# A three-layer Perceiver block on one core: self outputs moved one step on, the router a part later, the last key added first

## What is computed

```python
x = x + cross(layernorm(x), ctx, mask)     # softmax(Q K^T / 4, masked) V, with biases, then Wo
x = x + self_(layernorm(x))                # rope, causal softmax attention within a sequence, then W_O
h = layernorm(x)                           # the router and the experts read h
logits = h @ router_w                      # 8 experts, top 2, capacity 32 in groups of 128 tokens
x = x + combine(wo_e @ (gelu(w0_e @ dispatch(h)) * (w1_e @ dispatch(h))))
```

## Time and profile before

| | |
|---|---|
| median of 3 runs | 516.66 us (516.65 to 517.7) |
| the profiled execution | 520.1 us, of which the span from first to last instruction 518.3 |
| TensorE busy | 486.1 us, 94% |
| VectorE busy | 391.1 us, 75% |
| ScalarE busy | 323.0 us, 62% |
| GpSimd busy | 271.7 us, 52% |
| chain that ended last | TensorE 82%, VectorE 5%, ScalarE 4%, transfers 4%, issue 4% |

### The profile page before, as it was taken

One profiled execution on the slowest core, in us unless ns is written; L12 is line 12 of the kernel. 1 busy time (PEld: TensorE's weight loads), 2 busy tenths in 40 slices (PEclk: granted clock), 3 DMA queues, 4 the chain that ended last, 5 costly groups with the idle time before them and its releaser, 6 DMA issues.

```text
span 518.3 us, 18402 instructions
## 1 busy us (share of the span) xinstructions
PE 486.1 (94%) x6699; PEld 455.4 (88%) x6699; DVE 391.1 (75%) x987; ACT 323.0 (62%) x838; POOL 271.7 (52%) x362
## 2 busy tenths in 40 slices
PE   1898999899899999999998689999999999999997
PEld 1777889889889898998987679999999999999996
DVE  2544546476677768777679988999989999999984
ACT  1456776576667767776782356666667666666651
POOL 4125443445245464444544364998666666667660
PEclk9978999899899999999999997999999999999999
DMA  6614121111111111010005400556655646456302
GB/s 178 196 49 120 23 44 44 25 44 43 24 44 21 41 41 41 21 41 21 4 4 170 159 2 1 179 163 230 188 171 173 189 139 205 133 194 204 123 1 82
DMA packets 58126, 48.92 MB, mean 94 GB/s; under 512 B 20942, under 2 KB 49744, under 8 KB 58064
## 3 DMA queue, kind: packets, MB, share of 16 engines
q1 hardware_dynamic: 58064, 48.09, 31.7%
HBM read 46.86 MB, written 1.08 MB: 92 GB/s over the span
## 4 chain that ended last, share of the span: by engine, by line
PE 82%; DVE 5%; issue 4%; ACT 4%; DMA 4%; SPq 1%; DVEq 0%; POOL 0%; ACTq 0%; POOLq 0%
PE bank L226 20%; PE bank L228 19%; PE bank L227 19%; PE bank L647 4%; PE bank L669 3%; PE bank L615 3%; PE bank L572 3%; DMA ctx_raw<-in_ctx 2%; ACT Pr L1158 1%; DMA w_raw<-in_L_xattn_Wk 1%; PE bank L1054 1%; PE bank L933 1%; PE bank L805 1%; PE bank L765 1%; PE bank L537 1%
## 5 line engine op out<-in xcount | busy, mean ns | idle before, releaser
L226 PE MATMUL bank<-XT_lo,W_hi 128*128 128x256 f32 (+1 forms) x352 | 99.3, 282 | 0.3 <-DVE XT_lo L1934 0.3
L227 PE MATMUL bank<-XT_hi,W_lo 128*128 128x256 f32 (+1 forms) x352 | 99.0, 281 | 0.0
L228 PE MATMUL bank<-XT_hi,W_hi 128*128 128x256 f32 (+1 forms) x352 | 98.8, 281 | 0.0
L2337 POOL TENSOR_TENSOR W_lo<-raw,W_hi 128x256 fp32r<-128x256 f32 (+1 forms) x88 | 84.3, 958 | 7.0
L2219 POOL TENSOR_TENSOR Pr<-Pr,rinv 128x1028 f32<-128x1028 f32 (+2 forms) x32 | 60.4, 1889 | 49.2 <-DVE rinv L1514 48.5
L1158 ACT ACTIVATE Pr<-Sc,nmax 128x257 f32<-128x257 f32 x128 | 64.5, 505 | 29.3 <-DVE nmax L1503 24.8
L1974 DVE TENSOR_TENSOR W_lo<-raw,W_hi 128x512 fp32r<-128x512 f32 (+1 forms) x88 | 71.8, 817 | 4.9 <-ACT W_hi L1335 1.2
L2335 POOL CAST W_hi<-raw 128x256 fp32r<-128x256 f32 (+1 forms) x88 | 43.5, 494 | 53.4 <-PE bank L228 32.8
L1503 DVE CUSTOM_DVE_ANT_0 Sc<-bank,mask_add 128x257 f32<-128x257 f32 x128 | 47.0, 422 | 31.0 <-PE bank L615 17.4
L2146 DVE TENSOR_TENSOR hid_lo<-hid,hid_hi 128x256 fp32r<-128x256 f32 (+1 forms) x88 | 68.7, 781 | 1.5 <-ACT hid_hi L1410 1.5
L226 PEld LDWEIGHTS bank<-XT_lo,W_hi 128*128 128x128 f32 (+1 forms) x352 | 65.4, 186 | 0.4 <-issue 0.4
(11 more groups left out here) (248 smaller groups left out, 1342.8 us busy)
## 6 DMA issues: line engine op xcount, KB each, us to landing
raw<-in_L_ffn_w_kernel SPq DMA_DIRECT2D x32, 512.0 KB, 4.6
ctx_raw<-in_ctx SPq DMA_DIRECT2D x32, 256.0 KB, 2.8
raw<-in_L_ffn_wo_kernel SPq DMA_DIRECT2D x16, 512.0 KB, 5.7
raw<-in_L_ffn_w_kernel SPq DMA_DIRECT2D x16, 344.0 KB
last_prob<-Pr SPq DMA_DIRECT2D x128, 1.0 KB, 1.8
raw<-in_L_ffn_wo_kernel SPq DMA_DIRECT2D x8, 256.0 KB
x_sb<-in_x SPq DMA_DIRECT2D x4, 256.0 KB, 5.5
VL_all<-vl_rows SPq DMA_DIRECT2D x8, 128.0 KB
```

What stands on the lines that cost most here:

```text
L226: pe.matmul(dst, a_hi, b_lo, start=first, stop=False)
L227: pe.matmul(dst, a_lo, b_hi, start=False, stop=False)
L228: return pe.matmul(dst, a_hi, b_hi, start=False, stop=last)
L2337: po.tensor_tensor(W2_lo[0:w, m % RW, :], raw2[0:w, t, :], f(W2_hi[0:w, m % RW, :]), ALU.subtract)\
```

## The change

For tiles 0 to 4 it moves `self_outputs` from the end of part 3 to part 0 of the next step, behind `outputs`, with `split_self` on ScalarE and VectorE. `project_out` moves behind `keys` of that part, VectorE's addition and statistics behind `spread_queries`; y moves from part 0 to part 1, and with it `turn_router`, ScalarE's copy yTf and GpSimd's casts; the logits move from part 1 to part 2. `add_last` comes ahead of `invert_sums` in part 2 (and waits, for bank 7, for yTf instead of the logits). The waits of `outputs` follow these moves.

```diff
             if exists(t, TT):
-                for read in (("b_oT_hi", "b_oT_lo"), ("c_yT",), ("c_lg",))[(r + 2) % 4]:
-                    pe.wait_ge(sm[read], t + 1)
+                if r != 2:
+                    pe.wait_ge(sm[("c_yT", "c_lg", None, "b_x2")[r]], t + 1)
...
-                outputs(b - 2, (u - 2) % 4, j - 3 if u < 3 else -1)
+                outputs(b - 2, (u - 2) % 4, j - 3)
...
                 if u == 0:
-                    project_out(j - 3)
+                    self_outputs(j - 3)
...
                 if u == 0:
+                    project_out(j - 3)
                     turn_qk(j - 2)
                 if u == 1:
                     after_self(j - 2, True)
+                    turn_router(j - 3)
+                elif u == 2:
                     logits(j - 3)
-                elif u == 2:
                     project_cross(j - 1)
...
-                if u == 0:
-                    turn_router(j - 3)
-                elif u == 1:
+                if u == 1:
                     turn_last(j - 1)
-                elif u == 3:
-                    self_outputs(j - 2)
...
                 if u == 0:
                     keep_self_values(j - 2)
+                    split_self(j - 3)
...
-                if u == 1:
+                if u == 2:
                     keep_logits(j - 3)
                 keep_probs(b - 1, (u - 1) % 4)
-                if u == 0:
+                if u == 1:
                     keep_router(j - 3)
-                if u == 1:
                     self_exp(j - 2)
                     keep_last(j - 1)
-                if u == 3:
+                if ending:
                     split_self(j - 2)
...
-                ve.wait_ge(sm["c_lg"], min(t - 1, EARLY) if isinstance(t, int) else t - 1)
+                if isinstance(t, int) and t == TT - 1:
+                    ve.wait_ge(sm["c_lg"], EARLY)
+                else:
+                    ve.wait_ge(sm["c_yT"], t - 1)
...
-                invert_sums(b - 1, (u - 1) % 4)
                 if u == 2:
                     add_last(j - 1)
+                invert_sums(b - 1, (u - 1) % 4)
...
                 if u == 0:
-                    add_and_norm(j - 3, "c", 0)
+                    split_self(j - 3)
...
                 if u == 0:
+                    spread_queries(j - 2)
+                    add_and_norm(j - 3, "c", 0)
+                if u == 1:
                     add_and_norm(j - 3, "c", 1)
-                    spread_queries(j - 2)
-                if u == 1:
                     shift_scores(j - 2)
...
                     rotate(j - 1)
-                    split_self(j - 2)
...
                 if u == 0:
                     power(j - 3, "c")
+                elif u == 1:
                     keep_normed(j - 3)
```

## The result

The changed kernel takes 522.74 us (median of 14 runs), the kernel before, run with it, 517.24: a ratio of 1.011, 95% interval 1.0089 to 1.0132, some 5.5 us slower. The prediction was 518.8 (515.4 to 520.6): slower was right, the size was not, 2.1 us forecast where 5.5 came. The profiled execution took 523.45 us (span 521.7) where that of before took 520.1 (518.3).

A forecast was written before the change was run, and what follows sets the result against it. TensorE's stream was taken to bound the middle of the pipeline (busy 30.12 of 30.24 us). Terms -5.65 + 4.45 - 0.70 + 2.79 + 1.80 - 0.57 = +2.1 us on the median 516.66 gave 518.8, range 515.4 to 520.6.

The forecast's parts named there:

- the new wait for y: Part 1, steps 4 to 6: the router's transposes wait 0.93 us for VectorE's y, 3 x 0.93 = +2.79.
- Part 3 loses L805: Part 3, steps 2 to 6: the self outputs leave, with idle around them, 5 x -1.13 = -5.65 us.
- L805's place: Bounds on moving the self outputs from part 3 to part 0: -1.0 to +0.65 us on the sum.
- +0.89: Part 0: 1.01 for L805, -0.22 for the router transposes, +0.1 of waiting; five times, +4.45 us.
- The wait of project_out for O2T_lo: Part 0: TensorE waits 0.1 us for VectorE's O2T_lo, from 0 to 0.2.
- +0.17: Part 2 per step: gains the logits, 0.36 us, and loses the 0.19 wait for OT.
- The wait for OT: Part 2, before outputs (L669): the 0.19 us wait goes in three steps, -0.57; bound: it stays.
- one for PT (1.0): Part 1's outputs might wait for VectorE's late copy of PT: taken as 0, at most 0.2 us a step.
- half clock in steps 4 to 6: Rival: new waits are followed by half clock, 520.3 us for one such stretch, 523.3 for three; chance 0.09.
- wait-free version: Rival: the wait for y in part 1 isn't there, 516.0 us, or 515.0 with L805 at its lower bound; chance 0.12.
- the tail: Rival: after the pipeline, the half-clock stretch from 310.50 to 317.00 us doesn't occur, 515.5 us; chance 0.10.
- The gap of the first pass: Rival: the 1.90 us gap in part 1 of step 3 shrinks by 0.89 and the clock may hold, 517.3; chance 0.07.

The follow-up runs named there:

- The router's half alone: Kernel before with only y, its transposes, copies and casts moved to part 1 and the logits to part 2; self outputs stay: 521.08 us, ratio 1.0071.
- The pair of KT runs: ScalarE's KT made directly behind the spread self probabilities (PTd) in part 3: in the changed kernel 520.70 us, in the kernel before 516.69 us.
- last_T first: Kernel before with ScalarE's last_T made ahead of the exponential of the self scores in part 1: 517.89 us, ratio 1.0015.
- the run with that alone: Kernel before with only VectorE's addition of the last key moved ahead of the reciprocal of the sums: 517.79 us, ratio 1.0004.
- three kernels that keep the order of before on TensorE: Kernel before with one edit each: KT directly behind PTd 516.69 us, last_T ahead of the self exponential 517.89, the last key's addition ahead of the reciprocal 517.79.
- that and three other reorderings: Changed kernel with y ahead of the maxima, last_T ahead of the self exponential, KT behind PTd and O2T_hi ahead of the split context: 516.22 us.
- KT ahead of PTd: Changed kernel with ScalarE's KT made ahead of spreading the self probabilities (PTd) and the third exponential in part 3: 526.78 us, ratio 1.0164.
- KT behind PTd: Changed kernel with ScalarE's KT made directly behind PTd in part 3 of steps 2 to 6, ahead of the third exponential: 520.70 us, ratio 1.0066.
- O2T_hi alone: Changed kernel with ScalarE's O2T_hi made ahead of the split context instead of behind Vm in part 0: 521.44 us, ratio 1.0084.
- the trace with three edits: Changed kernel with y ahead of the maxima, KT ahead of PTd and O2T_hi ahead of the split context: 522.55 us, ratio 1.0099.

## Why the prediction was right and wrong

**Right: the new wait for y.** 0.93 was worked out from VectorE's row, 0.95 and 0.96 came, in steps 4 to 6 and only there, put down to y. Part 1 was to be 0.79 longer in these steps and was 0.76 to 0.81. The router's half alone has it as well, and y moved into VectorE's idle time ahead of the maxima takes it away.

**Wrong: the term "Part 3 loses L805", 5 x -1.13.** It measured -0.71 in a step, -0.63 in step 2: some -3.5 instead of -5.65, 2.1 us of the 3.4 missing. L805 was priced as if nothing lay under it. The next operand behind it, KT, was ready only 0.25 us after L805 had begun. Without L805 the values' products would have come 0.91 behind L647, at 181.63; KT ended at 182.00 and is seen some 0.05 later: 0.42 late, and -1.13 + 0.42 is the -0.71 that came. The trace of before had it, and it needed one look at what the instruction behind the removed one waits for; the bounds for "L805's place" had no such end. The pair of KT runs shows it.

**Too small: part 0, +1.13 in step 4 instead of +0.89.** Two sizes. The wait of project_out for O2T_lo is 0.19 to 0.24, not 0.1 (bound 0.2). And L805 stands 0.86, 0.84, 0.80, 0.81 and 0.69 behind L669 in steps 3 to 7, where other operations stand 0.70 behind it; I had taken no idle there. With 1.01 to the next instruction that is 1.1 a step, and part 3 without L805 and without the wait for KT is 7.34 to 7.37, 1.2 shorter. So moving L805 wins some 0.1 a step, as 1.13 less 1.01 said; each of the two was 0.1 too small. I had set aside a rule by which the idle would stay, and priced it at 0.6 us; the five distances give 0.5. The rule is that of the Trainium skill, "TensorE: Matmul & The Clock Gate", Part 3: a weight load overlaps running matmuls only when their row groups differ. The trace agrees for L805 in steps 3 to 6, but not in step 7, and not for L226 and L572, which use all rows as well and follow the same L669 without idle. So that this rule is the cause of the 0.1 isn't shown.

**Part 2, +0.25 instead of +0.17.** The logits came as priced. The wait for OT was worth 0.11 (6.98 to 6.86 with last_T first), not the 0.19 of the distance. That it goes in steps 4 to 6 was right, but the reason was mixed: VectorE's new order doesn't do it (nothing in the run with that alone), the wait for y does, by giving ScalarE time. Without that wait it is back, and larger.

**Steps 3 and 7.** No wait for y there, as said. But in part 2 of both L669 has 0.84 (put down to OT) and 0.80 of idle ahead, against 0.39 and 0.49 before, which no term had: 0.8 us in all.

**Range and chances.** The range left out the sum's high end (+6.8 on the median would be 523.5), which would have taken the 522.74 in. It would have done so by luck: its largest pieces, a wait for y in steps 3 and 7 (1.9) and one for PT (1.0), didn't come, and the wait for KT (2.1) lay in no bound. Nor were the waits independent: those for y, O2T_lo and KT all appear because TensorE's stream is made shorter ahead of a use or work is moved nearer to it. Of the rivals, there is no half clock in steps 4 to 6 and no wait-free version, and the tail still has its stretch at half clock. The gap of the first pass is shorter in the execution after, with no half clock behind; but it is about as short in three kernels that keep the order of before on TensorE (8.01 to 8.83 us for that part instead of 10.35), so the change isn't needed for it.

## What to carry to other kernels

Before pricing an instruction taken off the bounding engine, look up when the operands of the instruction behind it become ready: the win is only the time until the next of them is late. When a result and its use are moved into the same part, put the result into the idle time of its engine, ahead of what waits anyway; here that and three other reorderings turned 5.5 us of loss into none. And a reordering that takes one wait away should be followed to the next reader of each engine passed: KT ahead of PTd cost more than it gave.

## What the runs showed that was not expected

What TensorE does behind the cross outputs depends on the operation, without a settled cause: 0.69 to 0.94 us from L669 to L805 over 25 places in the traces of the changed kernel and four of its variants, against 0.69 to 0.74 from L669 to L226 or L572. And the half clock is no property of one version: the stretch near 310 us lasts some 7 us in most traces (3.4 us of half clock lost), but half as long in the changed kernel with KT behind PTd, with the router's half alone and with O2T_hi alone, and it isn't in the trace with three edits at all, without the cause being visible in the instructions.
